# Sixteen-head attention on Trainium2: scores four, then six pairs ahead, a later table load, and two queues for the first stores

## What is computed

```python
x = _layernorm(x + _L1_xattn_ref(ctx, ctx, x, mask, ...))   # masked
x = _layernorm(x + _L2_xattn_ref(ctx, x, mask, ...))        # masked, with a bias by distance
x = _layernorm(x + _L3_attn_ref(x, ...))                    # no mask, tokens regrouped
x = _layernorm(x + _L3_xattn_ref(x, ctx, ...))              # no mask
# the core of each: softmax(q @ k.T / sqrt(8) + mask) @ v, in float32, for 4 sequences and 16 heads
```

## Time and profile before

| | us |
|---|---|
| median of 3 runs | 1625.28 (1622.62 to 1627.15) |
| profiled execution, its own time | 1626.72 |
| span in its profile | 1624.9 |
| cores of the masked stages, start of the table load to last normalisation | 106.0 and 106.3 |
| core of the regrouped stage | 99.4 |
| core of the last unmasked stage | 86.1 |
| busy time: PE / DVE / ACT / POOL | 1230.5 / 989.4 / 880.4 / 511.8 |

### The profile page before, as it was taken

How to read it: one execution, slowest core, us unless ns; L and a number is a source line. 1 busy time by engine, 2 the same in 40 slices (tenths; PEclk the granted TensorE clock), 3 DMA queues, 4 the chain that set the end, 5 groups by cost and what they waited for, 6 DMA issues and landing times. The chain is left out here.

```text
span 1624.9 us, 20970 instructions
## 1 busy us (share of the span) xinstructions
PE 1230.5 (76%) x6984; PEld 616.4 (38%) x6984; DVE 989.4 (61%) x2012; ACT 880.4 (54%) x1816; POOL 511.8 (31%) x592
## 2 busy tenths in 40 slices
PE   8998647266666667976756987958867978979886
PEld 3674422022222224532323543433343433734452
DVE  3673455999999836622956634536435748737752
ACT  3773244699999835855024861234623745723643
POOL 0461004488888813200313100002101213503440
PEclk9999777599999997988977997987875989999998
DMA  3000000000000026001025200024115210000000
GB/s 145 2 2 3 20 9 0 1 0 1 0 0 1 0 98 130 2 33 39 0 82 120 41 1 17 0 50 98 21 54 115 43 54 1 1 0 1 1 2 13
DMA packets 43339, 48.74 MB, mean 30 GB/s; under 512 B 3040, under 2 KB 40032, under 8 KB 42080
## 3 DMA queue, kind: packets, MB, share of 16 engines
q1 hardware_dynamic: 43232, 47.40, 11.1%
HBM read 34.28 MB, written 13.11 MB: 29 GB/s over the span
## 5 line engine op out<-in xcount | busy, mean ns | idle before, releaser
L1408 POOL TENSOR_TENSOR L_attn_z<-L_attn_state,L_attn_r 128x1024 f32<-128x1024 f32 x64 | 151.1, 2361 | 21.3 <-DVE L_attn_state L1394 14.4
L1394 DVE TENSOR_TENSOR_SCAN L_attn_state<-bank,L_attn_w 128x512 f32<-128x512 f32 x128 | 148.9, 1204 | 0.0
L1305 PE MATMUL bank<-L_attn_z,const 128*128 128x512 f32 x256 | 139.4, 673 | 0.2 <-POOL L_attn_z L1412 0.2
L819 DVE CUSTOM_DVE_ANT_0 L_xattn_core_logits<-bank,L_xattn_mask 128x256 f32<-128x256 f32 x256 | 98.4, 422 | 54.3 <-PE bank L602 41.6
L1345 ACT ACTIVATE L_attn_r<-L_attn_after_dt,L_attn_half_guard,L_attn_A 128x512 f32<-128x512 f32 x128 | 96.5, 802 | 0.0
L1289 PE MATMUL bank<-L_attn_rows,L_attn_select 128*128 128x512 bf16 x96 | 36.3, 435 | 79.4 <-ACT L_attn_C L1357 42.7
L1335 ACT ACTIVATE bank<-L_attn_dt,L_attn_A 128x510 f32<-128x510 f32 x128 | 86.6, 676 | 12.5 <-DVE L_attn_state L1394 12.5
L731 ACT ACTIVATE L_xattn_core_probs<-bank 128x512 f32<-128x512 f32 x132 | 71.6, 596 | 38.0 <-PE bank L645 27.1
L602 PE MATMUL bank<-L_xattn_core_rows 48*128 48x256 bf16 x384 | 65.0, 314 | 29.5 <-DMA L_xattn_core_rows<-L_xattn_core_slots 15.6
L1412 POOL TENSOR_TENSOR L_attn_z<-L_attn_z,L_attn_C 128x1024 f32<-128x1024 f32 x32 | 75.8, 2369 | 23.3 <-ACT L_attn_C L1357 23.3
L1375 DVE TENSOR_TENSOR L_attn_w<-bank,L_attn_udt 128x1024 f32<-128x1024 f32 x64 | 78.2, 1221 | 5.0 <-PE bank L1289 1.6
(11 more groups left out here) (471 smaller groups left out, 3001.5 us busy)
## 6 DMA issues: line engine op xcount, KB each, us to landing
L_xattn_core_rows<-L_xattn_core_slots SPq DMA_DIRECT2D x24, 384.0 KB, 5.6
weights<-in_pack_L_ffn SPq DMA_DIRECT2D x2, 2118.5 KB, 8.4
L_xattn_core_slots<-L_xattn_core_k_parts SPq DMA_DIRECT2D x24, 128.0 KB, 2.0
L_attn_core_rows<-L_attn_core_slots SPq DMA_DIRECT2D x8, 384.0 KB, 6.2
weights<-in_pack_L_ffn SPq DMA_DIRECT2D x1, 2824.0 KB, 10.7
L_xattn_core_slots<-L_xattn_core_q_parts SPq DMA_DIRECT2D x12, 192.0 KB, 2.2
weights<-in_pack_L_xattn SPq DMA_DIRECT2D x1, 1539.5 KB, 6.4
weights<-in_pack_L_attn SPq DMA_DIRECT2D x2, 768.0 KB, 10.3
```

The source lines that it names most:

```text
L819: last = nc.vector.tensor_tensor_reduce(logits[:, c], scores_bank[side][:, c * S:(c + 1) * S], mask[:, 2 * b + c, :], 1.0, MASKED, ALU.add ...
L1305: last = nc.tensor.matmul(y_bank[2 * c + half][:], ident, z[:, g % NS, c], start=False, stop=False, skip_group_check=True)
L1394: nc.vector.tensor_tensor_scan(state[:, g % NS, c, ::step], a_bank[c][:, ::step], w[:, g % 2, c, ::step], 0.0, ALU.mult, ALU.add).then_inc ...
L1408: nc.gpsimd.tensor_tensor(z[:, g % NS], state[:, g % NS], r[:, g % NS], ALU.mult).then_inc(z_done, 1)
```

## The change

The scores' order on TensorE becomes a ramp. Scores 0 to 3 come first, then turn_shifts(0). For p from 0 to 5, shifted(p) is issued first, then scores up to 4 + p//2 ahead of the next pair, and the turning for the next quad moves from even to odd p. From p = 6 on, order and distance are as before. The table load moves behind ScalarE's rounding. In batch 0, ScalarE's queue issues the stores of q and SyncE's queue only those of k. In the regrouped stage the stores of batches 2 and 3 no longer wait for the rows of the batch before. TensorE runs two more warm-up matmuls once the stores of batch 0 have landed.

```diff
--- before.py
+++ after.py
@@ -494,7 +494,7 @@
     masked = mask is not None
     NP, NQ, LEAD = 2 * NG8 * B, NG8 * B, 6
     SPB = 2 * NG8
-    GATHER_AT, SUMS_AT, WARM = SPB + 3, SPB + 5, 4
+    GATHER_AT, SUMS_AT, WARM, LOADING, EARLY = SPB + 3, SPB + 5, 4, 2, 6
 
     with ExitStack() as stack:
         def sb(name, shape, dt=F32):
@@ -549,28 +549,28 @@
         def preloads(side):
             return masked and side == 1
 
+        def store(eng, b, n, part):
+            src = parts[n][:, part, tokens(b)]
+            for at in (SLOTS_K, SLOTS_Q)[n][part]:
+                if regrouped:
+                    for slot in range(6)[at]:
+                        eng.dma_start(slots[slot, :, :, b, n].rearrange("d h t -> h d t"), src).then_inc(stored[b], 16)
+                else:
+                    dst = slots[at, :, :, b, n].rearrange("s d h t -> (d h) s t")
+                    eng.dma_start(dst, src.unsqueeze(1).to_broadcast([P, dst.shape[1], S])).then_inc(stored[b], 16)
+
+        transfers = 12 if regrouped else sum(len(SLOTS_K[part]) + len(SLOTS_Q[part]) for part in range(3))
+
         @block.sync
         def _(sp):
             for b in range(B):
-                if b >= 1:
+                if b >= 1 and not (regrouped and b >= 2):
                     sp.wait_ge(rows_in[b - 1], 16 * 2)
-                count = 0
                 for part, ready in ((0, rounded), (1, rounded2), (2, split)):
-                    for n in (KEYS, QUERIES):
+                    for n in (KEYS,) if b == 0 else (KEYS, QUERIES):
                         sp.wait_ge(ready, 2 * b + n + 1)
-                        src = parts[n][:, part, tokens(b)]
-                        for at in (SLOTS_K, SLOTS_Q)[n][part]:
-                            if regrouped:
-                                for slot in range(6)[at]:
-                                    sp.dma_start(slots[slot, :, :, b, n].rearrange("d h t -> h d t"), src
-                                                 ).then_inc(stored[b], 16)
-                                    count += 1
-                            else:
-                                dst = slots[at, :, :, b, n].rearrange("s d h t -> (d h) s t")
-                                sp.dma_start(dst, src.unsqueeze(1).to_broadcast([P, dst.shape[1], S])
-                                             ).then_inc(stored[b], 16)
-                                count += 1
-                sp.wait_ge(stored[b], 16 * count)
+                        store(sp, b, n, part)
+                sp.wait_ge(stored[b], 16 * transfers)
                 for side in range(2):
                     sp.dma_start(rows[side_rows(side), :, b].rearrange("p h n t -> p h (n t)"),
                                  slots[:, :, 8 * side:8 * side + 8, b].rearrange("s d h n t -> (s d) h (n t)")
@@ -582,9 +582,10 @@
                 for at in (1, 3):
                     last = nc.tensor.matmul(shifted_bank[at][:], K.w("ident"), K.x[:, 0:HALF], start=True, stop=True)
                 last.then_inc(written, 1)
-            pe.wait_ge(split, 2)
-            for _ in range(WARM):
-                nc.tensor.matmul(out_bank[:], K.w("ident"), K.x[:, 0:HALF], start=True, stop=True)
+            for count, ready in ((WARM, (split, 2)), (LOADING, (stored[0], 16 * transfers))):
+                pe.wait_ge(*ready)
+                for _ in range(count):
+                    nc.tensor.matmul(out_bank[:], K.w("ident"), K.x[:, 0:HALF], start=True, stop=True)
 
             def row(n, side, p, c=None):
                 quad, t = divmod(p, 2)
@@ -672,13 +673,26 @@
                                             start=(half == 0), stop=(half == 1))
                 last.then_inc(sums_done, 1)
 
-            for p in range(-LEAD, NP + 3):
-                if p + LEAD < NP:
-                    scores(p + LEAD)
-                if 0 <= p < NP:
+            for p in range(LEAD - 2):
+                scores(p)
+            turn_shifts(0)
+            scored = LEAD - 2
+            for p in range(NP + 3):
+                ahead = min(NP, p + 1 + (LEAD if p >= EARLY else LEAD - 2 + p // 2))
+                if p >= EARLY:
+                    for scored in range(scored, ahead):
+                        scores(scored)
+                    scored = ahead
+                if p < NP:
                     shifted(p)
-                if p % 2 == 0 and 0 <= p // 2 + 1 < NQ:
-                    turn_shifts(p // 2 + 1)
+                if p < EARLY:
+                    for scored in range(scored, ahead):
+                        scores(scored)
+                    scored = ahead
+                if p % 2 == (1 if p < EARLY else 0):
+                    n = p // 2 + 1
+                    if n < NQ:
+                        turn_shifts(n)
                 if p % 2 == 1 and p >= 3 and (p - 3) // 2 % NG8 > 0:
                     values((p - 3) // 2, 0)
                 if p % 2 == 0 and p >= 4:
@@ -691,13 +705,20 @@
 
         @block.scalar
         def _(act):
-            nc.scalar.preload_act_table_set(LN_EXP)
             for b in range(B):
                 for i in (2 * b, 2 * b + 1):
                     nc.scalar.activation(piece(i, 0), piece(i), ACT.Copy).then_inc(rounded, 1)
+                if b == 0:
+                    act.wait_ge(rounded, QUERIES + 1)
+                    store(act, 0, QUERIES, 0)
                 for i in (2 * b, 2 * b + 1):
                     act.wait_ge(less, i + 1)
                     nc.scalar.activation(piece(i, 1), left(i), ACT.Copy).then_inc(rounded2, 1)
+                if b == 0:
+                    act.wait_ge(rounded2, QUERIES + 1)
+                    store(act, 0, QUERIES, 1)
+                    act.wait_ge(split, QUERIES + 1)
+                    store(act, 0, QUERIES, 2)
 
             def preload(p):
                 n, t = divmod(p, 2)
@@ -712,6 +733,8 @@
                 act.wait_ge(written, 1)
                 preload(0)
                 preload(1)
+
+            nc.scalar.preload_act_table_set(LN_EXP)
 
             def take_shifts(n):
                 act.wait_ge(shifts_done, n + 1)
```

## The result

| | before | after |
|---|---|---|
| median of the runs taken together | 1623.51 us (22 runs, 1618.04 to 1627.86) | 1629.5 us (22 runs, 1618.91 to 1641.36) |
| ratio after / before | | 1.0036, 95% interval 1.0019 to 1.0053 |
| profiled execution, own time | 1626.72 us | 1629.78 us |
| its span | 1624.9 us | 1627.9 us |

The changed kernel is slower by 0.36%, some 6 us (3 to 9 by the interval). The forecast was 1621.7 us: the sign was wrong, though the range, 1612 to 1631, held the time.

The account below looks back on a forecast made before the run. The bounds were taken to be the chain ahead of PE at each core's start and PE at half clock in the ramp. -10.6 (start) + 10 (masked ramps) + 1.5 - 4.5 = -3.6 us, median 1625.28 to 1621.7; range 1612 to 1631.

Parts of the forecast that it names:

- Start: Before first scores in all four cores: table move and q stores on ACT's queue bring rows earlier, together 10.6 us.
- Release of batches 2 and 3: Regrouped core: stores no longer wait for earlier rows, removing PE's wait at batch 3; 4.5 us gained (2 to 5.5).
- The three parts together: Table move, q stores on ACT's queue and release of batches 2 and 3: all but the ramp, -15.1 us.
- The ramp: TensorE's new order at each core's start: 5 us lost per masked core, 1.5 in the last, 0 in the regrouped.
- the masked terms: Ramp of the two masked cores: 5 us lost in each, the middle of 8 and 2 us late.
- The walk: Step-by-step timing from first scores (R) to pair 6: masked about 36 at half clock, regrouped 26 as before.
- The fast case: Masked cores' ramp: clock rises after pair 1 and stays, pair 6 near R + 30, 2 us late.
- the slow rival: Masked cores stay at half clock until values start, 9.5 us lost each: 1630.7 us; chance 0.15.
- The early clock: Clock rises early in masked cores, 2 us lost each, and the last core's ramp is free: 1614.2 us; chance 0.27.
- The late clock: Clock stays half in both masked cores until values start, near R + 30: +5.4 us, 1630.7; chance 0.15.
- ACT's queue: At the start ACT's queue saves nothing and batch 2's stores delay batch 1's rows, regrouped core: 1629.6 us; chance 0.12.
- The table: Program loads a table before the first rounding anyway, so the move does nothing: 1626.8 us; chance 0.08.

Follow-up runs that it names:

- ramp_undone: The changed kernel with TensorE's loop of the kernel before, everything else of the change kept: 1610.23 us, ratio 0.9925 to the kernel before.
- hold_ramp: The changed kernel, ramp included, with filler matmuls among the early scores and more warm-up matmuls to hold the clock: 1631.47 us, ratio 1.0033.
- table_alone: The kernel before with only the table load moved behind the rounding: 1619.33 us, ratio 0.9968.
- queue_alone: The kernel before with only batch 0's stores of q issued by ScalarE's queue: 1617.86 us, ratio 0.9967.
- release_alone: The kernel before with only the regrouped core's stores of batches 2 and 3 not waiting for earlier rows: 1623.58 us, ratio 0.9976.
- ramp_alone: The kernel before with only TensorE's new order from the changed kernel: 1637.51 us, ratio 1.0085.
- ramp_lead5: The changed kernel with four pairs of scores ahead for six pairs and five from then on: 1610.57 us, ratio 0.9928 to the kernel before.

## Why the prediction was wrong

**Start.** Forecast -10.6 us. The table's 5.1 hold (-5.2 alone). The 3.0 of the regrouped core hold (2.95). The 0.9 in each other core do not: 0.0 in the masked cores and 0.7 in the last one in this profile, some 0.4 in each over all profiles, with DMA engines that were nearly full. By this profile the start is worth 5.1 + 3.0 + 0.7 = 8.8.

**Release of batches 2 and 3.** Forecast -4.5. PE waits for no rows at batch 3 any more, and the half clock there is gone: in the changed kernel the clock is 1.00 from 1132 to 1150. Alone it gave -3.9, and 5.1 in its core's profile.

**The three parts together** were forecast at -15.1; with the ramp undone they gave -12.2, with an interval that holds -15.1.

**The ramp: the step that failed.** Its term in the sum was +11.5 us, two masked cores at 5 each and 1.5 in the last, and the sum of -3.6 needed an excess of only 3.6 us on it to lose its sign. Measured: about 18 by the ratios (13 to 23), 15.9 by the cores of the profiles, and 13.8 for the ramp alone, whose interval (8.6 to 19) still holds 11.5. By profile, from R to the end, changed kernel against ramp_undone: 97.1 against 92.0, 98.8 against 92.7, 78.5 against 76.9 and 74.2 against 71.9, or 5.1 + 6.1 + 1.6 + 2.3 = 15.1 us. So the masked terms were a little small, the last core's was 0.8 short, and the regrouped one, put at 0, has 1.6. The walk had its pair 6 at 26 "as before"; it came at R + 27.6, and the clock is 0.50 up to R + 31 (window of the kernel after, R is 1099.53); in ramp_undone it is 0.50 up to R + 25.

```profile
1100.00:1130.40 30.40, 24.15 (x166) 9.52 (x166) 18.01 (x28) 9.56 (x20) 5.37 (x24) 0.50 0.63 131
```

The mechanism of the masked term was not what ran, either. The prediction took the middle of two cases: the clock stays half (8 us late), or "rises after pair 1 and stays" (2 us late). What came was a third case. The clock rose at R + 12.9 and 11.0, and fell again at R + 23.1 and 17.9, amid and behind the stops for maxima that the walk itself had put at scores(7) and scores(10). Against the kernel before, the cores from R to the end then lost 4.4 and 5.9 us, close to the 5 forecast. That closeness is luck, because neither of the two averaged cases ran. The fast case itself is not contradicted. Pair 2 of the first core stands at 15.3, the next two pairs took 6.4 us at full clock, and the two after them take 8.4 in hold_ramp (9.0 less one filler's 0.6). That makes an estimate of 30.1 for pair 6, where the prediction said "near 30". What was wrong is the premise that the clock stays.

**The sum against the two profiles.** Start -8.8 (forecast -10.6), masked cores +10.3 (+10), regrouped core -2.7 (-4.5), last core +1.6 (+1.5): nothing gained and nothing lost, where -3.6 was forecast. The ratio's 6 us are more than that. A part may be that the kernel before drew a long masked core in its profile (R + 92.7 to its end, where table_alone, queue_alone and release_alone, in the same order, have 91.9); no profile shows the rest.

**What was right.** The walk's waits stand where it put them. At half clock pair 6 of the first masked core is 8.5 us late in ramp_alone (8 forecast). The number of the slow rival, 1630.7 us, is near the measured 1629.5, but not its mechanism: the clock did not stay half until the values came.

**Rivals.** The early clock: its condition came in both masked cores, but the clock did not stay, and its gain didn't come. The late clock: only in ramp_alone. ACT's queue: in part, 0.3 of 0.9 us in the rows load of a masked core; batch 1's rows were not held up. The table: did not return.

**What stays open.** Why two masked cores with the same instructions have their clock fall or not (ramp_lead5) no run here tells. How the loss divides between the waits and the clock is an estimate. And ratios and profiles differ: 18 against 15 us for the ramp, 6 against 0 for the whole change. Each profile is one execution, and those of the changed kernel spread from 1618.91 to 1641.36 us.

## What to carry to other kernels

A lead between two engines is filled at the pace of the slower one, and the faster one waits meanwhile. Starting with less of it moves that stop to a later place, where it interrupts the work and may cost the clock. So ask first how much lead the steady part needs (here five pairs do as well as six), and then build that at once. When a forecast averages a fast and a slow case of the clock, ask whether the work between them keeps the clock up: here it fell again. When filler work is used to hold the clock, put it in the same places in both kernels, off the path, or take its time out. A second DMA queue helps where issuing is the bound (twelve issues of 0.6 us, engines 37% busy: 3 us), and little where the engines are already near 90% busy (0.4 us).

## What the runs showed of the hardware

- A DMA issue on ACT's queue takes 0.42 to 0.51 us (0.61 to 0.66 regrouped), as on SP's.
- A 384 KB load followed at once by stores on the same queue was not slowed: 6.85 us, against 7.11 before (1105.62 to 1112.73 in the earlier trace rows).
- Filler matmuls meant to hold the clock held it in some cores. Where it fell they ran at half clock themselves, and the core was longer than the same core in ramp_undone: 99.5 against 92.7 us from R to the end in the second masked core, 87.2 against 71.9 in the last.
